# Output layer's tiles in another order, and the low parts of its input tiles made by VectorE, in a graph network kernel on one core

## What is computed

```python
# layer 0
neigh = segment_sum(x[src], dst, 1250)
rst = (1.0 + eps[0]) * x + neigh
h = maximum(rst @ W1 + b1, 0.0)          # the middle layer: 1250 x 1024
x = layernorm(x + (h @ W2 + b2 + x))     # the output layer: 1250 x 512
# four blocks
for i in range(4):
    y = cond_layer_norm(x, cond, ...)
    x = x + sparse_attention(y, src, dst, ...)     # softmax over the edges of a node
    y = cond_layer_norm(x, cond, ...)
    x = x + relu(y @ m_w1[i] + m_b1[i]) @ m_w2[i] + m_b2[i]
out = layernorm(x)
```

## Time and profile before

| what | value |
|---|---|
| median of 3 executions | 1796.01 us (1793.98 to 1800.16) |
| the profiled execution, its own time | 1803.08 us |
| its span, first to last instruction | 1801.3 us |
| mean granted TensorE clock | 0.988 of full speed |
| PE busy (TensorE matmul) | 1736.3 us, 96% |
| DVE busy (VectorE) | 1244.6 us, 69% |
| ACT busy (ScalarE) | 791.8 us, 44% |
| POOL busy (GpSimd) | 588.7 us, 33% |

### The profile page before, as it was taken

The page is one execution under the profiler, slowest core; times in us unless marked ns, Lnnn a source line. Parts: engine busy times, 40 slices in busy tenths (PEclk is TensorE's granted clock), DMA queues, the critical chain, the costliest instruction groups (busy, mean ns, idle before and its releaser), DMA issues.

```text
span 1801.3 us, 32290 instructions
## 1 busy us (share of the span) xinstructions
PE 1736.3 (96%) x11886; PEld 1529.9 (85%) x11886; DVE 1244.6 (69%) x2198; ACT 791.8 (44%) x1304; POOL 588.7 (33%) x892
## 2 busy tenths in 40 slices
PE   6999997899999999999999999999999999999998
PEld 5997786788999888879998888799987887999877
DVE  5998557736787668357776783577767835778676
ACT  4553432124666341246664412366644213666531
POOL 1003454402333534023334540123346401233383
PEclk9999998999999999999999999999999999999999
DMA  4002400221111212121212121211121122112221
GB/s 130 1 1 88 167 36 30 87 97 45 45 60 31 80 64 87 52 71 31 60 46 82 41 87 61 81 34 52 53 83 41 43 106 72 39 45 60 61 94 69
DMA packets 64714, 113.07 MB, mean 63 GB/s; under 512 B 15254, under 2 KB 25622, under 8 KB 64576
## 3 DMA queue, kind: packets, MB, share of 16 engines
q1 hardware_dynamic: 64576, 111.22, 19.1%
HBM read 89.19 MB, written 22.00 MB: 62 GB/s over the span
## 4 chain that ended last, share of the span: by engine, by line
PE 81%; DVE 10%; issue 4%; ACT 2%; DVEq 2%; POOL 1%; DMA 1%; SPq 0%; POOLq 0%; ACTq 0%
PE ps L1500 55%; PE ps L1561 14%; PE ps L1646 6%; PE ps L1587 2%; PE ps L1601 2%; DVE masked_s L1234 1%; DVE hot L1067 1%; DVE x L1271 1%; PE ps L1458 1%; DVE mask_log L1107 1%; DVE stat L1088 1%; DVE hot L1070 1%; DVE mask_out L1112 1%; ACT mask_log L857 1%; POOL rstd L637 1%
## 5 line engine op out<-in xcount | busy, mean ns | idle before, releaser
L1218 DVE TENSOR_TENSOR pT<-ps,pT 128x640 fp32r<-128x640 f32 (+1 forms) x320 | 243.9, 804 | 154.4 <-ACT pT L982 154.4
L1500 PE MATMUL ps<-yT,w 128*128 128x512 f32 (+1 forms) x1728 | 330.4, 352 | 1.3 <-DVE y L1355 1.3
L1500 PE MATMUL ps<-kh,q_parts 128*128 128x512 f32 (+3 forms) x1440 | 315.8, 363 | 10.2 <-DVE small L1234 7.0
L1500 PEld LDWEIGHTS ps<-yT,w 128*128 128x128 f32 x1728 | 280.5, 189 | 46.6 <-DVE y L1355 1.7
L982 ACT CAST pT<-ps 128x640 fp32r<-128x640 f32 (+1 forms) x320 | 202.4, 685 | 252.9 <-PE ps L1646 242.3
L1500 PEld LDWEIGHTS ps<-kh,q_parts 128*128 128x128 f32 (+1 forms) x1440 | 243.9, 185 | 58.2 <-issue 6.0
L1500 PE MATMUL ps<-w,kh 128*128 128x512 f32 (+1 forms) x960 | 240.5, 402 | 8.0 <-DVE x L1333 4.4
L1500 PEld LDWEIGHTS ps<-w,kh 128*128 128x128 f32 (+1 forms) x960 | 177.8, 190 | 48.4 <-DVE x L1333 5.3
L919 ACT ACTIVATE s<-masked_s,small 128x1280 f32 (+1 forms) x156 | 214.9, 1378 | 0.0
L1561 PE MATMUL ps<-pT,v 128*128 128x256 f32 (+1 forms) x1600 | 214.2, 280 | 0.0
L1561 PEld LDWEIGHTS ps<-pT,v 128*128 128x128 f32 x1600 | 199.5, 190 | 0.0
(11 more groups left out here) (188 smaller groups left out, 2596.2 us busy)
## 6 DMA issues: line engine op xcount, KB each, us to landing
mask<-mask_dram SPq DMA_DIRECT2D x24, 640.0 KB, 5.1
x_spill<-x SPq DMA_DIRECT2D x36, 256.0 KB
x<-x_spill SPq DMA_DIRECT2D x36, 256.0 KB, 4.6
rep<-rec_dram SPq DMA_DIRECT2D x64, 128.0 KB, 3.3
w_raw<-in_L_gnn_m_w_dram SPq DMA_DIRECT2D x8, 1024.0 KB, 6.0
mask_y<-mask_dram SPq DMA_DIRECT2D x12, 640.0 KB, 5.3
mask_dram<-mask_out SPq DMA_DIRECT2D x10, 640.0 KB, 2.9
x<-in_x_dram SPq DMA_DIRECT2D x2, 2304.0 KB
```

What stands on the lines that cost most here:

```text
L1218: nc.vector.tensor_tensor(pT[:, 1, places, k * P:k * P + R], turn_bank(half, R), pT[:, 0, places, k * P:k * P + R].bitcast(F32), ALU.subtr ...
L1500: mine = mm(to, left(a), right(b), start=first and n == 0, stop=final and n == 2)
```

## The change

1. **Order in the output layer.** The list for each i becomes: "Y" of tile i, "FS" and "FB" of i - 1, "T" of i - 3, and then "N0" of tile i.
2. **Low parts of the middle layer** (`hidden_low`), 10 subtractions of 128x1024: from GpSimd to VectorE. Tiles 0 and 1 come behind `w2_low_parts`, tile t + 2 behind the Y statistics of tile t. The four low parts of the first column group of `rst` go to VectorE too, behind the copies of neighbour sums 5 to 8.
3. **Masks.** ScalarE makes log(count + 1e-12) and 2e30 * count - 1e30 (an Identity with scale and bias), and VectorE takes the smaller: two operations on ScalarE and one on VectorE for a tile, in place of one and three.
4. **Attention without padding.** The last column group of the scores has 226 columns and not 256; mask, maximum and exponential run over 1250 columns and not 1280; the last tile's transposes load 98 columns of weights and not 128, and its `weigh` contracts over 98 rows and not 128. The clearing of the padding falls away.
5. **Start.** Only the first of the three table loads stands before the counting; the other two (and TensorE's load of the largest count) come behind the first quad. Two tiles of x are turned before the bounds and not four. ScalarE copies six of the turned tiles before the counting and four behind its first quad. The high part of x is ten casts, one in each counting block. The neighbour sums start before the last block of counts is copied out; only the fourth waits for it. Banks start at 6.
6. **Conditioning.** "C1" is four products of 80 columns and not two of 160; "C2" stands one product later.

```diff
     for n in range(QUARTERS - 1, -1, -1):
-        jobs = after(jobs, ("H", 1, 1), ("C2", n, 0))
-    for n in (1, 0):
+        jobs = after(jobs, ("H", 2, 1), ("C2", n, 0))
+    for n in range(QUARTERS - 1, -1, -1):
         jobs = after(jobs, ("H", 6, 0), ("C1", n, 0))
...
     for i in range(NT + 1):
-        mine = [(product, i, 0)] if i < NT else []
-        if product != "Y":
-            jobs += mine
-        elif i >= 1:
-            jobs.append(("N0", i - 1, 0))
+        if i < NT:
+            jobs.append((product, i, 0))
         if i >= 1:
             jobs += [("FS", i - 1, 0), ("FB", i - 1, 0)]
...
-        if product == "Y":
-            jobs += mine
+        if product == "Y" and i < NT:
+            jobs.append(("N0", i, 0))
...
-            for m in range(KD):
-                pool.wait_ge(rst_high_done, m + 1)
-                nc.gpsimd.tensor_tensor(rst_low[:, m, 0:GROUPS[0][1]], q[:, m, 0:GROUPS[0][1]], rst_high[0][:, m, :].bitcast(F32),
-                                        ALU.subtract).then_inc(rst_low_first, 1)
...
             for t in range(NT):
                 rstd_of(t, y_stats(t))
-                if t + 2 < NT:
-                    hidden_low(t + 2)
                 rstd_of(t, n0_stats(t))
...
+                if j == 0:
+                    for t in range(6, NT):
+                        turned_x(t)
+                    packed += load_edge_tiles(mybir.EngineType.Activation, LATER_LOADS)
                 if j:
                     counts_copy(j - 1, before)
+                nc.scalar.copy(x_high[0:rows(j), j, :], x[0:rows(j), j, :]).then_inc(x_high_done, 1)
...
-                nc.scalar.activation(mask_log[:, t % 2, :], mask_log[:, t % 2, :], ACT.Ln).then_inc(mask_ln, 1)
+                nc.scalar.activation(mask_log[:, t % 2, :], counts[:, t, :], ACT.Ln, bias=mask_consts[:, 0:1]).then_inc(mask_act, 1)
+                nc.scalar.activation(mask_out[:, t % 2, :], counts[:, t, :], ACT.Identity, bias=mask_consts[:, 1:2],
+                                     scale=-2.0 * NOTHING).then_inc(mask_act, 1)
...
+            def hidden_low(t):
+                R = rows(t)
+                dve.wait_ge(hid_high, t + 1)
+                nc.vector.tensor_tensor(hid[:, t % 2, 1, :, 0:R], hidden[:, :, t * P:t * P + R],
+                                        hid[:, t % 2, 0, :, 0:R].bitcast(F32), ALU.subtract).then_inc(hid_low, 1)
...
-                nc.vector.tensor_tensor_reduce(masked_of(u), ps_flat[0:R, 0:NP], masks[MASK_PLACE[t]][0:R, :],
+                nc.vector.tensor_tensor_reduce(masked_of(u), ps_flat[0:R, 0:N], masks[MASK_PLACE[t]][0:R, 0:N],
...
                         stats(a, y_stats(a))
+                        if a + 2 < NT:
+                            hidden_low(a + 2)
...
-            pe.wait_ge(counts_out, NT + 2)
+            most_quads = most[0]
+            pe.wait_ge(counts_out, NT + 1)
...
-                for b, (c0, cn) in enumerate(((0, 512), (512, 512), (1024, 256))):
+                for b, (c0, cn) in enumerate(GROUPS):
...
-                                mine = nc.tensor.transpose(turn[:, t - tiles[0], :].bitcast(F32R),
-                                                           s_of(u)[:, t * P:(t + 1) * P].bitcast(F32R), ident_r[0:R, 0:R])
+                                mine = nc.tensor.transpose(turn[0:rows(t), t - tiles[0], :].bitcast(F32R),
+                                                           s_of(u)[:, t * P:t * P + rows(t)].bitcast(F32R), ident_r[0:R, 0:R])
```

146 lines of the change are left out of this document (75 added, 71 removed).

## The result

| | before | after |
|---|---|---|
| median of four executions each | 1794.99 us | 1769.72 us (1768.15 to 1772.59) |
| the profiled execution, its own time | 1803.08 us | 1772.59 us |
| its span | 1801.3 us | 1770.9 us |

The ratio of after to before is 0.9857, with a 95% interval of 0.9836 to 0.9878: the change saves 25.3 us, and by that interval 22 to 29. The width comes mostly of the kernel before. Over all rounds of this case its executions lie between 1793.86 and 1803.95 us and its medians between 1794.92 and 1798.86. The profiled execution of before lay 8.1 us above its median, that of after 2.9 us, so the two traces differ by more, 30.4 us.

What follows compares the result with a forecast made beforehand. TensorE was taken as busy nearly throughout most stretches before attention, but waiting on GpSimd in the output layer. Terms -19.4 - 3.3 - 0.6 - 3.8 + 0.5 = -26.6 us, from median 1796.01, give 1769.4; range 1757 to 1780.

Steps and rivals of the forecast that it cites:

- output layer: Order and low parts changed in the output layer: waits for GpSimd go, gain 19.4 us, bounds 11 to 21.
- second neighbour sum: Neighbour sums: the second product begins 0.3 us behind the last low part of x, gain 3.3 us.
- pause behind the sums: TensorE's 2.89 us pause after the neighbour sums: inferred to be the jump over their second copy, so kept, no gain.
- middle layer: Middle layer: C2 one product later removes TensorE's idle time, gain 0.6 us, bounds 0 and 0.7.
- attention and behind: Attention: 480 matmuls at 226 columns and not 256, 8 ns each, gain 3.8 us; upper bound 6.7.
- start: Counting stage: earlier start against a second slow quad and added ScalarE casts, cost 0.5 us, bounds -2 and +3.
- friction: Output layer: 1.6 us added for VectorE and TensorE at the same load, giving 58.5 us.
- Rival A: Output layer: VectorE becomes the bound; at 7.5 us a round the gain is 11 us, time 1778; chance 0.13.
- Rival B: After the neighbour sums: the 2.89 us pause was a wait and goes, 4.5 us more gain, 1765; chance 0.12.
- the bound of -5.3: Attention, last tile's transposes: load shrinks with its columns, 33 ns less, -5.3 us over 160 units; other end +3.7, taken 0.
- the transfer of 8 ns: Attention: each matmul of 226 columns and not 256 saves 8 ns (119 against 111), 480 times, 3.8 us.
- Rival C: Counting stage falls to half clock through ScalarE's casts: 1.6 us a quad, 80 us over 49, 1849; chance 0.02.

## Why the prediction was right, point by point

The forecast was 1769; it is 1769.72. By its own steps, in the traces:

| step | predicted | traces |
|---|---|---|
| output layer | -19.4 | -21.6 |
| second neighbour sum | -3.3 | -1.3 (-3.2 against the low parts of x, +1.9 from the start) |
| pause behind the sums | 0 | -1.4 |
| middle layer | -0.6 | -2.2 |
| attention and behind | -3.8 | -3.9 |
| start | +0.5 | +1.9, held in the second row |
| sum | -26.6 | -30.4 |

The two profiled executions stand 8.1 and 2.9 us above their medians, so 5.2 us of the traces' difference belong to them and not to the change; the difference of the medians, 25.3, is 1.3 less than forecast. In which stages the 5.2 us lie is open. It isn't the output layer, which took 79.65 us again in a kernel that was traced at its median, nor the units of attention, which repeat to 0.001 us. That leaves 0.5 us of the medians' difference for all the other rows, which make 5.6 in the traces. So the output layer is forecast well and for the right reason. That the whole came out within 1 us is in part luck: the other terms miss by up to 2 us each, in both directions, and the median of before alone moves by 4 us between rounds.

**Output layer.** The mechanism was right in all that the text asked to see: no wait for the roots but 0.8 us, the norm at 0.54, the subtraction at 1.19, no wait ahead of Y, the clock at 1.00. The term that was mis-sized is the friction: 1.6 us were added for two engines at equal load, and there was none. VectorE's rounds came to 52.7 us busy in 58.0, TensorE's to 58.0. A round on TensorE is 6.46 us (291.13 to 297.59 in its timeline), as the working had it (6.01 + 0.4). The other 0.6 us are TensorE's own: from the end of Y 0 to the end of Y 9 it needs 56.3 us and not 56.9, mostly since six groups of transposes and not seven stand in between. What the text did not say is that the two parts largely take away the same waits: it argued from GpSimd's 2.17 us as a cause of its own, and with the new order it is worth 1.7 us. Rival A did not come.

**Neighbour sums.** "The second product begins 0.3 us behind the last low part": it began 0.4 behind (the low parts end at 139.88 + 6.11 = 145.99). In all traces of kernels with the new start it is 0.4. The low parts themselves were later by 1.9 us, which belongs to the start.

```profile
139.88 6.11 DVE L1090 TENSOR_TENSOR x_low<-x,x_high 128x512 fp32r<-128x512 f32 x10
```

**The pause.** It stayed, at 1.51 and not 2.89 us, and it belongs to the branch, as inferred: with the branch taken out, it is gone. That it would shrink was not foreseen. In the kernels with the branch it was 1.3 to 2.9 us (2.9 in the two that start from before, 1.3 to 2.3 in the others), and why it varies stays open. Rival B, a wait, falls.

**Middle layer.** Predicted 0.6 for the wait in front of C2, which is gone. The other 1.6 are the slow matmuls behind the pause. Before, eight of them stand 0.43 us apart, and the granted clock from 192 to 196 us is 0.57; after the shorter pause they stand 0.23 us apart, and it is 1.00. The text had put them into rival B alone. Of the 4.5 us that rival B promised, 3.0 came in the traces, without its wait.

**Attention.** 3.8 against 3.2 in the units (0.0201 x 160), but not by the parts as written. The transposes, taken at nothing, gave 2.0 us (0.0122 x 160): the true value lay on the side of the bound of -5.3, since the load shrinks with its columns, though by 14 ns and not 33. The contraction over 98 rows, not costed, took 0.5. What is left for the scores is 3.2 - 2.0 + 0.5 = 1.7 us, 3.6 ns a matmul and not 8: the step that failed is the transfer of 8 ns from matmuls of `weigh` to those of the scores. This 1.7 is a remainder, which no run measured by itself. Errors of opposite sign cancelled here.

**Start.** 1.9 us lost in this trace, within the bounds. Its two halves are larger than thought: the first block ended 2.4 us earlier (38.87 against 41.26), and the nine boundaries cost 4.3 us. The first half is the unsteady one. In the seven kernels with this start the low parts of x are ready between 142.24 and 145.99 us, in the middle at 145.1, against 144.0 and 144.1 in the two traces with the old start. So the usual loss is 1.0 us, nearer to the 0.5 predicted, and the 1.9 are this trace's own. What the text mis-sized here is the slow stretch behind the first quad, "up to 1.6 us": from the end of TensorE's pause to the end of the first block it is 12.8 us in the kernel after and 10.0 where the clock stayed at 1.00, a cost of 2.8 us. The prediction named the place ("each right where it is also to copy counts") and did not price it. Rival C did not come: the clock of the stage is 0.97 as before, and 1.00 from 40 us on.

## What to carry to other kernels

Before an operation is moved to another engine to take it out of a wait, see whether the wait needs it: here a new order of one list took away the same waits and gave 19.9 of 21.6 us. Look whether small work can stand in the middle of another engine's period and not at its boundary, where several things fall together: here a cast of 0.62 us cost 0.5 us at each boundary and nothing in four pieces inside. Where medians vary by more than the question, measure a period over many repeats in one trace: it resolved 0.003 us a unit. And where a trace is compared with one other, see first how far kernels with the same code differ in that stretch: the counting stage moved by 3.7 us without any edit there.

## What the runs showed of the hardware that was not expected

VectorE and GpSimd shut each other out while certain instructions run. VectorE's norm of 512 columns takes 0.54 us alone. In the kernel before, where GpSimd's subtraction starts 0.06 to 0.08 us ahead of it, it takes 2.4 us in seven rounds of nine and ends 0.3 us behind the subtraction each time:

```profile
262.11 2.21 POOL L669 TENSOR_TENSOR hid<-hidden,hid 128x1024 fp32r<-128x1024 f32 x1
262.19 2.41 DVE L1271 TENSOR_SCALAR x<-x,mv,rstd 128x512 f32<-128x512 f32 x1 [1.13 <-POOL rstd L637]
```

The other way round, GpSimd's one-column L641 takes 0.21 us alone and 0.99 beside VectorE's subtraction of 1.20. VectorE's instructions with one operand in PSUM are not stretched: the y rows take 743 to 748 ns in all four combinations, and with the low parts on GpSimd and the new order a yT row of 0.68 us lies wholly inside GpSimd's subtraction:

```profile
272.06 2.20 POOL L677 TENSOR_TENSOR hid<-hidden,hid 128x1024 fp32r<-128x1024 f32 x1
...
272.39 0.68 DVE L1307 TENSOR_TENSOR yT<-ps,yT 128x512 fp32r<-128x512 f32 x1
...
273.00 1.54 DVE L1281 TENSOR_SCALAR x<-x,mv,rstd 128x512 f32<-128x512 f32 x1
```

The Trainium skill (SBUF — State Buffer, section Who interferes with whom) has this as an exclusive lock on a pair of ports that both engines share: a VectorE instruction in a two-port mode, or one with two SBUF inputs beside a GpSimd instruction that reads SBUF, contends with the GpSimd instruction, and whichever starts first holds the pair to its end. The traces agree with it; whether the norm runs in a two-port mode, no row shows. The prediction saw one direction of it in the earlier trace rows and missed the other: work on VectorE in front of a wait for GpSimd covers nothing if it locks GpSimd out.
